# Attention scores of two fp32 parts on halves of the TensorE array, two places at a time, with stack rows on every third partition

## What is computed

```python
k = proj(W_key)      # [b, 16 heads, 512, 16], scaled
q = proj(W_query)
scores = jnp.einsum('bhqd,bhkd->bhqk', q, k) * hd ** (-0.5)
scores = jnp.where(causal, scores, -jnp.inf)
weight = jax.nn.softmax(scores, axis=-1)
out = jnp.einsum('bhqk,bhkd->bhqd', weight, v)
```

## Time and profile before

| | us |
|---|---|
| median of 3 runs (lowest, highest) | 906.53 (905.8, 908.62) |
| the profiled execution | 912.49 |
| its span in the trace | 910.7 |
| PE busy, share of the span | 818.5, 90% |
| DVE busy, share of the span | 601.3, 66% |
| ACT busy, share of the span | 533.2, 59% |
| POOL busy, share of the span | 472.5, 52% |
| L776 `nat` on PE, 512 matmuls | 125.6 |
| L761 `st` on PE, 512 matmuls | 126.1 |
| L625 maxima on DVE, 512 | 238.8 |

### The profile page before, as it was taken

One profiled execution on the slowest core, in us unless ns is written; L12 is line 12 of the kernel. 1 busy time (PEld: TensorE's weight loads), 2 busy tenths in 40 slices (PEclk: granted clock), 3 DMA queues, 4 the chain that ended last, 5 costly groups with the idle time before them and its releaser, 6 DMA issues.

```text
span 910.7 us, 17163 instructions
## 1 busy us (share of the span) xinstructions
PE 818.5 (90%) x5876; PEld 612.6 (67%) x5876; DVE 601.3 (66%) x2059; ACT 533.2 (59%) x1048; POOL 472.5 (52%) x642
## 2 busy tenths in 40 slices
PE   4658999999999999997778999999999999999990
PEld 3434445454545445342348999999999999999990
DVE  4457787878877778898957854546464544636464
ACT  2225676758676766665748545546465656555554
POOL 6336575665556566333748446544444444435243
PEclk9778999999999999998899999999999999999995
DMA  4999686767686876910055223435243342523158
GB/s 139 167 142 180 104 153 104 146 122 150 121 155 116 153 129 120 217 53 25 22 193 169 36 30 59 96 80 139 45 94 75 55 125 44 143 31 58 20 142 262
DMA packets 89991, 100.52 MB, mean 110 GB/s; under 512 B 8625, under 2 KB 83377, under 8 KB 89777
## 3 DMA queue, kind: packets, MB, share of 16 engines
q1 hardware_dynamic: 72448, 77.92, 40.8%
q0 software_dynamic: 12800, 16.92, 11.5%
q10 hardware_dynamic: 4656, 4.59, 1.5%
HBM read 65.38 MB, written 33.62 MB: 109 GB/s over the span
## 4 chain that ended last, share of the span: by engine, by line
PE 70%; DVE 13%; ACT 6%; DMA 5%; issue 3%; SPq 2%; POOL 1%; ACTq 0%; POOLq 0%; DVEq 0%
PE y_ps L1358 21%; PE h_ps L1344 19%; PE av_ps L793 7%; PE st_ps L761 5%; DVE n_ps L625 5%; PE n_ps L776 4%; PE stage_ps L810 3%; PE stage_ps L818 3%; PE stage_ps L852 3%; DMA part_d<-w_raw 2%; PE tp_ps L1317 2%; ACT pt L523 1%; DVE nmax L625 1%; SPq L397 1%; PE stage_ps L843 1%
## 5 line engine op out<-in xcount | busy, mean ns | idle before, releaser
L625 DVE CUSTOM_DVE_ANT_0 n_ps<-n_ps,tri 128x512 f32<-128x512 f32 (+3 forms) x512 | 238.8, 519 | 85.3 <-PE n_ps L776 83.6
L523 ACT ACTIVATE pt<-st_ps 128x512 f32<-128x512 f32 x320 | 184.5, 602 | 64.7 <-PE st_ps L761 49.4
L1358 PE MATMUL y_ps<-w_parts,h_hi 128*128 128x256 f32 (+1 forms) x1152 | 215.2, 281 | 2.1 <-issue 1.5
L1178 ACT ACTIVATE g<-h_ps,b 128x384 f32<-128x384 f32 (+1 forms) x192 | 104.1, 542 | 162.2 <-PE h_ps L1344 144.1
L1358 PEld LDWEIGHTS y_ps<-w_parts,h_hi 128*128 128x128 f32 (+1 forms) x1152 | 172.5, 177 | 6.0 <-issue 1.8
L1150 POOL DMA_INDIRECT acc<-y,tok_no x64 | 103.1, 1611 | 139.7 <-DVE y L1293 130.0
L1344 PE MATMUL h_ps<-tt_hi,w_parts 128*128 128x384 f32 (+1 forms) x768 | 169.7, 323 | 3.7 <-issue 2.0
L1279 DVE TENSOR_TENSOR h_lo<-g,h_hi 128x384 fp32r<-128x384 f32 (+1 forms) x176 | 90.4, 514 | 118.4 <-ACT h_hi L1183 98.2
L452 POOL TENSOR_SCALAR_AFFINE_SELECT pt<-pt 128x256 f32<-128x256 f32 (+1 forms) x320 | 109.9, 361 | 108.7 <-ACT pt L523 108.0
L1358 PE MATMUL y_ps<-w_parts,h_lo 128*128 128x256 f32 (+1 forms) x576 | 161.5, 280 | 0.0
L761 PE MATMUL st_ps<-w_parts 99*128 99x512 bf16 (+3 forms) x512 | 126.1, 308 | 16.8 <-ACT pt L523 14.6
(11 more groups left out here) (192 smaller groups left out, 1075.7 us busy)
## 6 DMA issues: line engine op xcount, KB each, us to landing
w_parts<-part_d SPq DMA_DIRECT2D x192, 128.0 KB, 6.3
w_raw<-in_w SPq DMA_DIRECT2D x16, 1024.0 KB
part_d<-w_raw SPq DMA_DIRECT2D x96, 128.0 KB, 6.3
w_raw<-in_xt SPq DMA_DIRECT2D x8, 512.0 KB, 5.3
res<-in_x SPq DMA_DIRECT2D x8, 512.0 KB, 11.4
x<-res SPq DMA_DIRECT2D x8, 512.0 KB, 3.2
acc<-res SPq DMA_DIRECT2D x8, 512.0 KB, 5.2
fin<-acc SPq DMA_DIRECT2D x4, 512.0 KB, 3.9
```

Source lines behind the costliest of these rows:

```text
L523: nc.scalar.activation(pt[:, slot % PT_RING, n % UP, :], st_ps[at % ST_RING][:, :], ACT.Exp, scale=S_SCALE).then_inc(exp_done, 1)
L625: ins = nc.vector.tensor_tensor_reduce(out=src[:, h, :], in0=src[:, h, :], in1=mask, scale=-1.0, scalar=-BIG_NEG, op0=ALU.add, op1=ALU.min ...
L1178: nc.scalar.activation(g[:, at % G_RING, 0:cols], h_ps[at % H_RING][:, 0:cols], ACT.Gelu, bias=b1[:, e, n:n + 1]).then_inc(g_done, 1)
L1358: ins = nc.tensor.matmul(y_ps[at % Y_RING][0:rows, 0:C], x[:, q % 2, m, toks], w[e % 2][:, m, :], start=i == 0, stop=i == len(terms) - 1)
```

## The change

Keys and queries are cut into two parts of rounded fp32 (F32R) instead of three of bf16. Three blocks of 16 rows instead of six hold the products that count (48 rows), the maxima and the ones take two rows instead of three (50 rows for `st`). Each head now lies in the lower or the upper 64 partitions: heads 0 and 1 below, 2 and 3 above, and so on, and a matmul uses that half of the array alone. `nat` units are made of the two heads of a pair whose half is the other one than that of the `st` unit of the same place. `steps()` yields two places together: st, nat, st, nat, then the `av` of both, then the stages of the first and the second. The rows of a block lie on every third partition of its half, the three blocks interleaved. The weight columns are reordered on the host accordingly. The cores of the diff:

```diff
-K_PARTS = (0, 0, 1, 1, 0, 2)
-Q_PARTS = (0, 1, 0, 1, 2, 0)
-BLOCKS = len(K_PARTS) + len(Q_PARTS)
+K_PARTS = (0, 1, 0)
+Q_PARTS = (0, 0, 1)
+GROUP = P // 2
+BLOCKS = 2 * (len(K_PARTS) + len(Q_PARTS))
 KQ = len(K_PARTS) * D
-KM = KQ + 3
+KM = KQ + 2
+def place_of(h):
+    return h // 2 % 2, h // 4 * 2 + h % 2
+def rows_for(h, rows):
+    first = place_of(h)[0] * GROUP
+    return slice(first, first + rows), place_of(h)[1]
...
-N_UNITS = [(qb, h - heads + 1, heads) for h in range(H) for qb, heads in ((3, 1), (2, 1), (1, 2), (0, 4)) if (h + 1) % heads == 0]
+N_PAIR = (((0, 3, 0),), ((1, 3, 0),), ((0, 2, 0), (0, 0, 384)), ((1, 2, 0), (1, 0, 384)), ((0, 1, 0), (1, 1, 256)))
+N_UNITS = [[(2 * (slot ^ 1) + h, qb, c) for h, qb, c in unit] for slot in range(PAIRS) for unit in N_PAIR]
...
-                if 0 <= i < B:
-                    yield "st", i, (2 * g) * UP + k
-                if 0 <= nat_b < B:
-                    for n in range(N_QUARTER * k // 10, N_QUARTER * (k + 1) // 10):
-                        yield "nat", nat_b, nat_0 + n
                 group = i * GROUPS + g - 1
-                if k in AV_PLACES and 0 <= group < B * GROUPS:
-                    yield "av", group, AV_PLACES.index(k)
+                for at in (k, k + 1) if k % 2 == 0 else ():
+                    if 0 <= i < B:
+                        yield "st", i, (2 * g) * UP + at
+                    if 0 <= nat_b < B:
+                        for n in range(N_QUARTER * at // 10, N_QUARTER * (at + 1) // 10):
+                            yield "nat", nat_b, nat_0 + n
+                for at in (k, k + 1) if k % 2 == 0 else ():
+                    if at in AV_PLACES and 0 <= group < B * GROUPS:
+                        yield "av", group, AV_PLACES.index(at)
...
+        sp.wait_ge(ones_ready, 1)
+        for first in (0, GROUP):
+            dst = kst_b[first + KQ:first + KM, :, :, :].rearrange("p a h n -> p (a h) n")
+            sp.dma_start(dst, ones[:, :].bitcast(BF16).unsqueeze(1).to_broadcast([KM - KQ, 2 * HH, 2 * T])).then_inc(ones_in, 16)
...
-                for part in range(3):
-                    sp.dma_start(part_d[which, b % 2, part, half_, :, :], parts[:, tile % 2, part, :]).then_inc(parts_out[tile % 2], 16)
+                for part in range(2):
+                    sp.dma_start(part_d[which, b % 2, part, half_, :, :], parts[:, tile % 2, part, :].bitcast(BF16)).then_inc(parts_out[tile % 2], 16)
...
                     for at, part in enumerate(blocks):
-                        src = part_d[which, b % 2, part, n, :, :].rearrange("(h d) n -> d h n", d=D)
-                        sp.dma_start(stack[at * D:(at + 1) * D, b % 2, HH * n:HH * (n + 1), :], src).then_inc(stack_in[n][b % 2], 16)
+                        for first in (0, GROUP):
+                            src = part_d[which, b % 2, part, n, first:first + GROUP, :].rearrange("(h d) n -> d h n", d=D)
+                            sp.dma_start(stack[first + at:first + KQ:len(blocks), b % 2, HH // 2 * n:HH // 2 * (n + 1), :],
+                                         src).then_inc(stack_in[n][b % 2], 16)
...
-                link(nc.gpsimd.tensor_tensor(qk_r[:, :], qk_f[:, tile % 2, :], parts[:, tile % 2, 0, :], ALU.subtract))
-                link(nc.gpsimd.tensor_tensor(parts[:, tile % 2, 1, :], qk_f[:, tile % 2, :], parts[:, tile % 2, 0, :], ALU.subtract))
-                nc.gpsimd.tensor_tensor(parts[:, tile % 2, 2, :], qk_r[:, :], parts[:, tile % 2, 1, :], ALU.subtract).then_inc(qk_rest, 1)
+                nc.gpsimd.tensor_tensor(parts_r[:, tile % 2, 1, :], qk_f[:, tile % 2, :], parts[:, tile % 2, 0, :], ALU.subtract).then_inc(qk_rest, 1)
...
-                    nc.gpsimd.memset(kst[KQ:KM, :, :, :].rearrange("p a h n -> p (a h n)").bitcast(F32), two_ones).then_inc(consts, 1)
...
-                act.dma_start(qst[KQ:KM, b % 2, HH * n:HH * (n + 1), :], nmt[:, :]).then_inc(rows_in, 16)
+                for group in range(2):
+                    act.dma_start(qst_b[group * GROUP + KQ:group * GROUP + KM, b % 2, HH // 2 * n:HH // 2 * (n + 1), :],
+                                  nmt[HH * group:HH * (group + 1), :].bitcast(BF16)).then_inc(rows_in, 16)
...
-                link(nc.vector.tensor_copy(nm3[:, :, 0, :], mine))
-                link(nc.vector.tensor_tensor(nmax_r[:, :, :], mine, nm3[:, :, 0, :], ALU.subtract))
-                link(nc.vector.tensor_copy(nm3[:, :, 1, :], nmax_r[:, :, :]))
-                nc.vector.tensor_tensor(nm3[:, :, 2, :], nmax_r[:, :, :], nm3[:, :, 1, :], ALU.subtract).then_inc(nm_parts, 1)
+                link(nc.vector.tensor_copy(nm2[:, :, :, 0, :].bitcast(F32R), mine))
+                nc.vector.tensor_tensor(nm2[:, :, :, 1, :].bitcast(F32R), mine, nm2[:, :, :, 0, :], ALU.subtract).then_inc(nm_parts, 1)
...
                 for hh, kb, c in ST_UNITS[u]:
-                    h = 2 * pair + hh
-                    ins = nc.tensor.matmul(st_ps[at % ST_RING][:, c:c + T - kb * P], kst[0:KM, b % 2, h, kb * P:(kb + 1) * P],
-                                           qst[0:KM, b % 2, h, kb * P:T], start=True, stop=True)
+                    rows, slot = rows_for(2 * pair + hh, KM)
+                    ins = nc.tensor.matmul(st_ps[at % ST_RING][:, c:c + T - kb * P], kst[rows, b % 2, slot, kb * P:(kb + 1) * P],
+                                           qst[rows, b % 2, slot, kb * P:T], start=True, stop=True)
```

More of the change, by code:

```diff
@@ L29 @@
 O_SCALE = float(C) ** -0.5 * float(C) ** -0.5
-K_PARTS = (0, 0, 1, 1, 0, 2)
-Q_PARTS = (0, 1, 0, 1, 2, 0)
-BLOCKS = len(K_PARTS) + len(Q_PARTS)
+K_PARTS = (0, 1, 0)
+Q_PARTS = (0, 0, 1)
+GROUP = P // 2
+BLOCKS = 2 * (len(K_PARTS) + len(Q_PARTS))
 KQ = len(K_PARTS) * D
-KM = KQ + 3
+KM = KQ + 2
[4 more added lines that the diff above has]
+    return slice(first, first + rows), place_of(h)[1]
+HEAD_ORDER = [8 * n + 4 * quarter + 2 * group + h for n in range(2) for group in range(2) for quarter in range(2) for h in range(2)]
 ST_UNITS = (((0, 0, 0),), ((0, 1, 0), (0, 3, 384)), ((0, 2, 0), (1, 2, 256)), ((1, 0, 0),), ((1, 1, 0), (1, 3, 384)))
@@ L426, in link @@
             pool.wait_ge(pool_step, made[0])
+        nc.gpsimd.memset(ones[:, :], 1.0).then_inc(ones_ready, 1)
         link(nc.gpsimd.memset(ident[:, :], 0.0))
-        link(nc.gpsimd.affine_select(out=ident[:, :], in_=ident[:, :], compare_op=ALU.not_equal, fill=1.0, base=0,
-                                     pattern=[[-1, P]], channel_multiplier=1))
-        nc.gpsimd.tensor_copy(ident_b[:, :], ident[:, :]).then_inc(consts, 1)
+        nc.gpsimd.affine_select(out=ident[:, :], in_=ident[:, :], compare_op=ALU.not_equal, fill=1.0, base=0,
+                                pattern=[[-1, P]], channel_multiplier=1).then_inc(consts, 1)
         nc.gpsimd.memset(mean_of[:, :], 1.0 / C).then_inc(rw_mean, 1)
@@ L552, in _ @@
                     act.wait_ge(qk_rest, tile - 1)
-                    act.wait_ge(parts_out[tile % 2], 48 * (tile // 2))
-                nc.scalar.activation(parts[:, tile % 2, 0, :], ps[:, :], ACT.Copy).then_inc(qk_first, 1)
+                    act.wait_ge(parts_out[tile % 2], 32 * (tile // 2))
+                nc.scalar.activation(parts_r[:, tile % 2, 0, :], ps[:, :], ACT.Copy).then_inc(qk_first, 1)
                 nc.scalar.activation(qk_f[:, tile % 2, :], ps[:, :], ACT.Copy).then_inc(act_free, 1)
@@ L615, in _ @@
             if stage == "nat":
-                qb, h0, heads = N_UNITS[n]
                 at = b * NU + n
@@ L621, in _ @@
                     dve.wait_ge(consts, 2)
-                src = n_ps[at % N_RING][:, 0:heads * (qb + 1) * P].rearrange("p (h k) -> p h k", h=heads)
-                mask = tri[:, 3 - qb:4, :].rearrange("p a k -> p (a k)")
-                for h in range(heads):
-                    ins = nc.vector.tensor_tensor_reduce(out=src[:, h, :], in0=src[:, h, :], in1=mask, scale=-1.0, scalar=-BIG_NEG,
-                                                         op0=ALU.add, op1=ALU.min, accum_out=nmax[:, b % 2, qb, h0 + h:h0 + h + 1])
+                for h, qb, c in N_UNITS[n]:
+                    src = n_ps[at % N_RING][:, c:c + (qb + 1) * P]
+                    mask = tri[:, 3 - qb:4, :].rearrange("p a k -> p (a k)")
+                    col = HEAD_ORDER.index(h)
+                    ins = nc.vector.tensor_tensor_reduce(out=src, in0=src, in1=mask, scale=-1.0, scalar=-BIG_NEG,
+                                                         op0=ALU.add, op1=ALU.min, accum_out=nmax[:, b % 2, qb, col:col + 1])
                 ins.then_inc(max_done, 1)
@@ L772, in _ @@
                     pe.wait_ge(max_done, at - N_RING + 1)
-                bank, w = n_ps[at % N_RING], (qb + 1) * P
-                for j in range(heads):
-                    h = h0 + j
-                    ins = nc.tensor.matmul(bank[:, j * w:(j + 1) * w], qst[0:KQ, b % 2, h, qb * P:(qb + 1) * P],
-                                           kst[0:KQ, b % 2, h, 0:w], start=True, stop=True)
+                for h, qb, c in N_UNITS[n]:
```

(8 more changed lines are left out.)

49 lines of the change are left out of this document (23 added, 26 removed).

## The result

The kernel after takes **935.98 us** (median of 4 runs, 933.9 to 936.97), the kernel before on the same chip 907.33 (905.8 to 908.62): a ratio of **1.031, 95% interval 1.029 to 1.033**. Forecast were 894 us and a range of 876 to 916, so both are wrong, and the sign too. The profiled executions differ by 24.5 us (spans of 935.2 and 910.7).

The account below looks back on a forecast made before the run. DMA landings were taken to bound the start, TensorE the steady sequences. Start -10 us and steady part -3 us (-0.6 per sequence over six, less projection waits), from the median 906.53, gave 894 us; range 876 to 916.

Parts of the forecast that it names:

- The start: Before the first `st`: spread stack transfers land sooner and VectorE does fewer subtractions; -10 us, ends 0 and -14.
- Term (1): `st` and `nat` of a place overlap on opposite halves: a pair takes 0.60 us for 0.89, -4.1 us per sequence.
- term (2): Visits to `av` fall from 16 to 8 per sequence, saving switch time going in and out: -1.8 us.
- Rival C: `st` and `nat`: halves don't overlap, or narrow fp32 matmuls take several passes; +24 us, 918 us, chance 14%.
- B: Rival: weight loads of the two halves go one after the other, 0.755 us per pair; +13, 907 us, chance 12%.
- Term (3): New switches between half-array and full-array matmuls, plus uncovered weight loads: +3.7 us per sequence, ends 0 and +4.5.
- Term (4): Third group: ScalarE's new order makes PE wait 2.2 us before place 8, where it waited 0.32: +1.9 us per sequence.
- (5): Maxima in two fp32 parts need two VectorE operations for four, so PE's 0.35 us wait goes: -0.3 us.
- the projections: Projections in neighbouring places may wait longer for VectorE to free their two banks: 0.1 us per sequence.
- exps set the pace as now: Where no `av` or stages cover a pair's exps (1.0 us), they were to set the pace unchanged; no cost.
- rival E: The clock falls where PE now waits, once per sequence, some 2.2 us at half speed; +13, 907 us, chance 10%.
- The prediction's own sign of being wrong: Pairs of places at 0.75 us or more, landings as before, or granted clock below 1 between 100 and 380 us.

Follow-up runs that it names:

- (a): The kernel before with the spread rows and, on top, the `av` of two places in one visit: 911.6 us, ratio 1.003.
- both with fillers: The kernel after with useless matmuls before each `st` of group 3, once with 128 rows and once with 48: 946.93 and 934.6 us.
- the run on one half: The kernel after with `nat` of a place on the same half as its `st`, so they follow one another: 971.05 us, ratio 1.067.

## Why the prediction was wrong

**The start, -10 us: right in mechanism, half lost.** Alone the spread gives 9.5 us at the first `st`. In the kernel after it is 5.5, and at the first projection (140.2 against 139.4 us) nothing is left. The step that failed is the one that let `st` wait only for the stack's landing and VectorE's maxima: PE itself became the chain, at a clock of 0.62 from 30 to 60 us (spread alone: 0.73). 11 us of the miss lie here.

The Trainium skill's page "SBUF — State Buffer", section "Door 1: The DMA port swizzle", by which the rate goes with the number of ports that the partitions reach, stood beside this step; the trace agrees, 6.3 us to landing against 2.7 with only the partitions changed.

**Term (1), the overlap, -4.1: right in mechanism.** The pair takes 0.71 us where 0.49 + 0.54 stood; forecast were 0.60 and a switch of 0.2 in front of it. The parts lie otherwise: `nat` didn't wait for the last matmul of `st` (both start at 315.23), and the bare load of the switch is inside the 0.71. That the sums agree (0.60 + 0.2 forecast, 0.71 and 0.09 in front of it measured) is in part luck. Of the 0.32 us saved, 0.09 is the way into one visit to `av`, which term (2) counts. Rival C is out. So is B: the weight loads of the two halves start together (PEld, 315.22 for `st` and 315.23 for `nat`), and behind the first matmul 384 columns take 0.18 us (315.57 to 315.75), no longer than at 0.235 for 512.

**Term (2), fewer visits, -1.8: right in size, but not a gain by itself.** 256 and 128 columns together take 0.79 us for 0.57 + 0.36, so 0.14 per visit is saved on the way out, and the 0.09 on the way in lies in the pair above. But in full rows the saving turns into waits (a).

**Term (3), the switches, +3.7: right in price where it can be read.** On the way in `st` starts 0.33 us after the last two products of `v` (318.06 to 318.39), before 0.24, and the first 512 columns on a half take 0.34 us for 0.235: together the forecast 0.2. PE's work fell by more than the 2.2 us of the three terms; they count 14 of 20 pairs, and the other six, in which PE waits, shrank as well (0.89 to 0.71 us, an estimate of 1 us per sequence).

**Term (4), ScalarE's order, +1.9: right at its place, too small in all.** The wait before place 8 is 2.03 us (forecast 2.2). But all idle time of PE grew by 3.2 us per sequence; the net forecast of terms (4), (5) and the projections was 1.7. The rings "hold one pair" and so "exps set the pace as now" failed: a pair of exps takes 1.07 us and a pair of places now 0.71, so PE waits behind pairs that no stage follows, as 0.97 us at 321.74.

**The clock: the step that decided.** The step of the prediction that failed is its sum, which puts the clock at nothing; it priced it as rival E alone, once per sequence, 2.2 us, and tied it to waits. It costs 4.9 to 5.8 us per sequence and comes mostly with the matmuls on fewer rows: 0.87 with 48 rows and 0.95 with 64 and 66, all with almost no waits, 1.00 with 96, and 0.98 with 128 rows and 21.6 us of waits. Waits seem to take a smaller part: with full rows in twos, 30.5 us of them go with 0.96, and the kernel after has 30.6. The prediction's own sign of being wrong, a clock below 1 between 100 and 380 us, was the one that came.

Summed per sequence: work -3.9 (forecast -2.2), waits +3.2 (+1.7), clock +4.9 (0), together +4.2 for -0.5 (level by level, work -4.8 and clock +5.8). From the first to the fifth projection that is 16.8 us measured where -2 was forecast; the sequences after it, forecast at about 0, lose another 7.3 (clock 0.84 from 390 to 490 us, before 0.91).

What stays open: why fewer rows lower the clock, why the clock with halves that overlap (0.90) lies where it does between the runs with 48 and 66 rows although two of them together fill 98 rows at once, and why the kernel after, the one in single places, both with fillers and the one with 64 rows all settle at 54.6 to 54.8 us per sequence though their work differs.

## What to carry to other kernels

A matmul on fewer rows is not cheaper where TensorE sets the pace: its time goes by columns (0.23 us for 512 columns with 48 rows, 0.22 with 96), and the clock granted to the whole stretch may fall with the rows, for the full-array work beside it as well. Before an array is halved so that two matmuls can overlap, run the kernel with the row slices cut and nothing else; that one run would have shown the loss here. Where ScalarE or VectorE is slower in some places than TensorE (a pair of exps takes 1.07 us, a pair of places 0.71), work saved on TensorE comes back there as waits, and small moves that shorten the others (an issue on another queue) are worth more.

## What the hardware showed that was not expected

- The granted clock falls while TensorE is busy: 48 rows, PE busy 291.6 of 300 us, clock 0.87. The Trainium skill's page "TensorE: Matmul & The Clock Gate", section "Part 1: The HAM clock gate", ties the clock to how busy PE has been. The trace agrees only in part: in twos with full rows waits go with 0.96, but with 48 rows the busier run has the lower clock, and there the measurement decides.
- The first fp32 matmul of 512 columns on a half takes 0.34 us behind a stage, the next 0.24 (318.14 and 318.48 in the run on one half), about one weight load more; in bf16 with 48 rows the first takes 0.23 as well.
- Going from the full array into a half costs about 0.09 us in front of the first matmul: 0.34 us from the last two products of `v` to `st` with 64 rows, 0.24 with full rows.
